# A GpSimd fill of 400 columns in place of 900 between pairs of indirect transfers

## The reference

```python
x = x + 0.5 * ffn(layernorm(x), gate_w, gate_b, w1, b1, w2, b2)
x = x + attn(layernorm(x), Wq, Wkv_down, Wk_up, Wv_up, Wo)
x = x + 0.5 * ffn(layernorm(x), gate_w, gate_b, w1, b1, w2, b2)

def ffn(x, ...):                      # 8 experts, 2 of them for each token
    probs = softmax(x @ gate_w.T + gate_b)
    topk_vals, topk_idx = top_k(probs, 2)
    h = relu(einsum('bsd,edh->bseh', x, w1) + b1)      # 256 hidden units
    expert_out = einsum('bseh,eho->bseo', h, w2) + b2
    return sum(expert_out[topk_idx] * topk_vals)

def attn(x, ...):                     # 8 heads of 32 features, softmax over 512 keys
    ...
```

## Time and profile before

| | us |
|---|---|
| median of 3 runs | 1219.44 |
| lowest and highest | 1216.77 and 1219.60 |
| the profiled execution | 1225.29 |
| its span, first to last instruction | 1223.5 |
| busy: PE | 1150.6 |
| busy: ACT | 958.0 |
| busy: DVE | 724.7 |
| busy: POOL | 678.9 |

### The profile page before, as it was taken

One profiled execution on the slowest core, in us unless ns is written; L12 is line 12 of the kernel. 1 busy time (PEld: TensorE's weight loads), 2 busy tenths in 40 slices (PEclk: granted clock), 3 DMA queues, 4 the chain that ended last, 5 costly groups with the idle time before them and its releaser, 6 DMA issues.

```text
span 1223.5 us, 25810 instructions
## 1 busy us (share of the span) xinstructions
PE 1150.6 (94%) x8142; PEld 762.4 (62%) x8142; DVE 724.7 (59%) x2254; ACT 958.0 (78%) x2383; POOL 678.9 (55%) x768
## 2 busy tenths in 40 slices
PE   7989898999989989999999999999999999999896
PEld 3666576666666545676666665665766446667575
DVE  4775438666496745665555867555756636647245
ACT  4457748789898898997888888898989888888532
POOL 2035548537370887803876777881820884257646
PEclk8977888799999979999999998999999989999988
DMA  8056546456574115655677645567652144676872
GB/s 279 10 206 192 162 144 193 126 156 202 158 214 147 55 39 177 208 172 157 200 215 228 194 139 164 186 201 206 183 157 60 41 151 125 182 214 176 250 253 80
DMA packets 159882, 202.05 MB, mean 165 GB/s; under 512 B 16938, under 2 KB 103426, under 8 KB 159747
## 3 DMA queue, kind: packets, MB, share of 16 engines
q1 hardware_dynamic: 144196, 168.90, 44.8%
q0 software_dynamic: 15360, 31.49, 8.9%
q10 hardware_dynamic: 192, 0.02, 0.0%
HBM read 152.50 MB, written 47.84 MB: 164 GB/s over the span
## 4 chain that ended last, share of the span: by engine, by line
PE 68%; ACT 20%; DVE 4%; issue 3%; POOL 3%; DMA 2%; SPq 0%; POOLq 0%; ACTq 0%; DVEq 0%
PE psum L1568 63%; ACT probs L1173 7%; ACT psum L1182 6%; PE psum L1686 2%; DVE neg_m L1522 2%; POOL Y L1100 2%; ACT xnC L1138 1%; DMA wt<-packed 1%; ACT xnA L1138 1%; PE psum L1653 1%; ACT hg L1219 1%; POOL pause L1064 1%; ACT xnB L1138 1%; PE psum L1751 1%; ACT xg_T L1247 1%
## 5 line engine op out<-in xcount | busy, mean ns | idle before, releaser
L1522 DVE TENSOR_REDUCE neg_m<-psum 128x1 f32<-128x512 f32 x512 | 317.5, 685 | 189.4 <-PE psum L1568 188.9
L1568 PE MATMUL psum<-nat 32*128 32x512 f32 x2048 | 372.7, 667 | 2.8 <-ACT nat L1251 1.5
L1182 ACT ACTIVATE psum<-psum,neg_m 128x512 f32<-128x512 f32 x512 | 340.9, 681 | 34.5 <-DVE neg_m L1522 33.7
L1173 ACT ACTIVATE probs<-psum 128x512 f32<-128x512 f32 x512 | 266.0, 627 | 37.7 <-PE psum L1568 36.4
L1080 POOL DMA_INDIRECT slots_A<-xnA,posA x120 | 117.1, 976 | 197.9 <-DMA xs<-slots_A 64.3
L1100 POOL DMA_INDIRECT Y<-results_C,posC x120 | 115.4, 962 | 170.8 <-DMA results_C<-ys 130.9
L1064 POOL MEMSET pause<- 128x900 f32 x240 | 207.6, 865 | 0.1
L1568 PEld LDWEIGHTS psum<-xg_T,wt 128*128 128x128 f32 x1296 | 163.6, 200 | 49.7 <-ACT psum L1182 14.7
L1568 PEld LDWEIGHTS psum<-nat 32*128 32x128 f32 x2048 | 135.7, 191 | 91.7 <-issue 22.1
L1568 PE MATMUL psum<-xg_T,wt 128*128 128x128 f32 x1296 | 180.2, 290 | 7.4 <-DMA wt<-packed 3.3
L1568 PEld LDWEIGHTS psum<-wt,hg 128*128 128x128 f32 x1296 | 153.0, 193 | 27.6 <-ACT hg L1219 9.6
(11 more groups left out here) (190 smaller groups left out, 1374.9 us busy)
## 6 DMA issues: line engine op xcount, KB each, us to landing
wt<-packed SPq DMA_DIRECT2D x324, 320.0 KB, 4.0
xs<-slots_A SPq DMA_DIRECT2D x36, 256.0 KB, 4.3
results_A<-ys SPq DMA_DIRECT2D x36, 256.0 KB
xs<-slots_C SPq DMA_DIRECT2D x36, 256.0 KB, 4.4
results_C<-ys SPq DMA_DIRECT2D x36, 256.0 KB
X<-in_L_attn_x_dram SPq DMA_DIRECT2D x16, 256.0 KB, 8.0
out_dram<-X SPq DMA_DIRECT2D x16, 256.0 KB, 3.9
packed<-probs SPq DMA_DIRECT2D x1, 2560.0 KB, 9.0
```

Source lines behind the costliest of these rows:

```text
L1173: act.activation(probs[:, kt, j, :], at.banks()[j][:], ACT.Exp).then_inc(a_done, 1)
L1182: act.activation(at.banks()[j][:], at.banks()[j][:], ACT.Exp, bias=neg_m[:, g, n, j:j + 1], accum_out=sums[:, g, n, j:j + 1]).then_inc(S[" ...
L1522: V_.tensor_reduce(neg_m[:, g, n, j:j + 1], at.banks()[j][:], AX.X, ALU.max, negate=True).then_inc(S["r_done"], 1)
L1568: return nc.tensor.matmul(dst, w, m, start=start, stop=stop)
```

## The change

The tile that `apart` fills has 400 columns instead of 900. The fill, the wait on its end, the order of all steps and every other wait stay as they are; the rows of PE, DVE and ACT are the same in both programs, and on POOL only the width of the fill differs.

```diff
         ident = sb("ident", [P, P])
-        pause = sb("pause", [P, 900])
+        pause = sb("pause", [P, 400])
         ones = sb("ones", [P, P])
```

## The result

| | before | changed |
|---|---|---|
| median, lowest to highest, us | 1219.52 (1216.77 to 1221.9, 4 runs) | 1212.24 (1211.77 to 1212.77, 4 runs) |
| ratio, 95% interval | | 0.9941 (0.9920 to 0.9963) |
| profiled execution, its span, us | 1225.29, 1223.5 | 1212.48, 1210.7 |
| mean granted clock of TensorE | 0.946 | 0.954 |
| the changed kernel once more, later, median, us | 1219.59 (33 runs) | 1215.43 (12 runs) |

The change makes the kernel faster, by 7.3 us in the first comparison and by 4.2 us in the second (0.5 to 7.8 us by the interval). The forecast was 2.5 us. Its range held both times; its likeliest outcome, the same, did not come. Four executions in the slow state are left out of all medians and ratios of the later comparisons.

The account below looks back on a forecast made before the run. PE was taken to bound the kernel, with 68% of the chain (POOL 3%). Terms of 1.45 and 1.0 us sum to 2.5 us less, 1219.44 to 1216.9 us; own range 1214.5 to 1219.0, wider range 1211.0 to 1222.5 us.

Parts of the forecast that it names:

- likeliest outcome, the same: Whole kernel: time between 1215.8 and 1223.1 us, not told from no change; chance 0.58.
- The fill and the pace: On POOL: fill 0.43 us shorter, its row 0.42 to 0.45 us; pace of pairs from 3.35 to 2.92 us.
- The rival that the pace does not change: On POOL: pairs held by their own transfers, whose rows grow by what the fill loses; 1219.4 us, chance 0.06.
- The first term, the end of the program: Last gather steps: gathers done 4.7 us earlier, but DVE's dense sum lets the last `comb` start only 1.45 us earlier.
- The part of the step on the last store of `results_C`: Last four gathers may wait for this store until 1201.7 us; last transfer still lands at 1214.7 us, ahead of DVE's 1215.24.
- The second term, the operations that the fill holds up: Small DVE operations on the chain held by transfer and fill: 1.0 us less, bounds 0 and 3.7 us.
- The square rule: DVE holds: lost time goes with the square of the hold's length, 1.4 to 0.95 us, leaving 0.46.
- the prediction's reading of the row at 878 us: DVE operation beside a first transfer of a pair, no fill directly behind: takes 0.17 us, so is not held.
- the halving: Holds on the chain: half of the 2.0 us taken, 1.0 us, since the second latest input may take over.
- the rows at 608 us: DVE operation of 1.40 us, starting 0.46 us into a second transfer, ending with the fill behind; read as the longer hold.
- The rivals on the clock: PE's low-clock stretch from 208 us disappears, 1211.4 us, chance 0.15; or a new one comes at 192 us, 1224.0 us, 0.13.
- The prediction's sign of being wrong: Longer indirect transfers, DVE still waiting at the end for gathered rows, or over 4 us change with the clock as it was.

Follow-up runs that it names:

- 900 columns and no holds: DVE's small one-operand operations rewritten with two tile operands, fill kept at 900 columns, against the kernel before: 1216.35 us, ratio 0.9964.

## Why the prediction was right in its range and short in its sum

**The fill and the pace** came as worked out: 448 ns, which is the value taken down from the 900 columns, and 2.93 us for the forecast's 2.92 us, with the transfers' rows unchanged. The rival that the pace does not change is out.

**The first term, the end of the program, was mis-sized: 1.45 us were forecast, 3.2 to 3.5 us measured.** The step that the prediction took was right as far as it went: the idle time of 1.47 us ahead of the last `comb` is gone, and DVE's own work is what is late next. What it missed is that the last row on the chain of waits is not the end of the program. The span ended with POOL's DRAIN, 2.2 us after SP had everything; with the faster POOL the DRAIN ends 1.0 us ahead of SP. So POOL's whole end counts down to the point where SP's takes over. In the two traces the end part is 4.6 us shorter: 1.5 us of DVE's idle time, 2.0 us (2.2 − 0.2) of SP's wait for the DRAIN, and the remaining 1.1 us because the dense sequence ended that much earlier after the last `shiftC`, which is scatter or a held operation less. The first two make 3.5 us, and 400 columns at the end alone took 3.2 ± 1.3 us less at equal clock. The other kernels confirm it on both sides: with 900 columns at the end alone the end part is 61.6 us again, 1300 bring it to 65 and 66 us with POOL last, and from 500 columns down it stops falling, since SP is last. The part of the step on the last store of `results_C` was right too: the last gathers wait 1.4 us for it, and it costs nothing.

**The second term, the operations that the fill holds up, came out larger as well: 1.0 us was forecast, 1.9 to 2.8 us are the best values measured.** The mechanism was right: with 900 columns and no holds the time falls by 1.9 ± 1.3 us at equal clock, with 1300 by 5.6 ± 1.6 us. That 1.0 us was too small is likely but not shown, since it lies inside the first interval (0.6 to 3.1 us). One factor of the term was wrong for certain, the share of held time that is left. The square rule with (0.95 / 1.4)² gave 46%; the traces show 6.9 of 33.9 us, 20%. The rule took the hold to run through the last half microsecond of the transfer and then the fill. With 900 columns it does; with 400 an operation caught in the transfer is let go at the transfer's end. At 187 us of the changed kernel:

```profile
187.20 0.97 POOL L1080 DMA_INDIRECT slots_A<-xnA,posA  x1 [0.31 <-issue]
187.44 0.69 DVE L1354 TENSOR_SCALAR shiftA<-shiftA 128x4 f32<-128x4 f32 x1
188.16 0.45 POOL L1064 MEMSET pause<- 128x400 f32 x1
```

It ends at 188.13 us, where the fill only begins. So there are two short windows in the place of one long one: 0.69 − 0.17 = 0.52 us in the transfer, and the fill's 0.45 us. The same square rule with them gives (0.52² + 0.45²) / (1.58 − 0.17)² = 24%, close to the 20% measured. The rule was sound, and its 0.95 us was wrong. (A first transfer of a pair holds too, against the prediction's reading of the row at 878 us: in before, 8 of the 50 held operations start 0.53 us or more after the start of a first transfer and end with it. The row at 878 us starts after 0.42 us.)

The other factor is what a hold on the chain is worth. The prediction counted four of them, 3.7 us, and halved what the rule said would go. On the chain of the changed kernel three such pieces of more than 0.3 us are left:

```profile
336.91 0.66 DVE neg_hl L1541
...
452.30 0.35 DVE neg_hl L1541
...
1101.08 0.50 DVE shiftC L1354
```

They hold 1.0 us, where before has 3.7 us in the prediction's four and 0.4 us in two shorter ones (at 203 and 340 us), so the chain gave up 3.1 us. With 80% of 3.7 us gone, the halving would make 1.5 us and no halving 3.0 us; the 1.9 ± 1.3 us at equal clock fits either, and the 2.8 us of the fit the second. So whether the halving was right stays open. Counted by all held time instead of by the chain, a held microsecond costs 0.06 to 0.12 us at equal clock (1.9 of 33.9 us, 5.6 of 48.6 us), and 0.10 us by the fit.

The terms measured add up to 5 to 6 us. The four kernels with 400 columns or fewer throughout show 3.7 to 4.6 us at equal clock, with 1.2 to 1.6 us to either side, so one term or both may lie at the low end. The first comparison's 7.3 us holds some 3 us more, which go with its four executions at a high clock. As far as these runs show, that is luck and not the change.

**The rule of the Trainium skill** ("SBUF — State Buffer", section "Who interferes with whom"), that whoever comes first keeps the shared ports for its whole instruction, would have left a quarter of the lost time if the fill alone held DVE. The prediction weighed that against the longer hold in the rows at 608 us and went by the rows. With 400 columns the measured 20% is nearer to that rule's quarter than to the 46%: there, a fill holds up only what comes during it or just ahead of it, though the transfer holds as well. At 900 columns the rule by itself does not describe the rows, as a hold passes from the transfer into the fill. On which operations are held the traces agree with it: casts and tensor-scalar operations took up to 1.58 us, and none of the 166 is held in the two-operand form.

**The rivals on the clock** did not come at the places given for them. The changed kernel's windows around 192 and 208 us, beside the earlier trace rows:

```profile
192.00:196.00 4.00, 4.00 (x39) 3.96 (x41) 0.88 (x2) 3.70 (x12) 3.21 (x4) 1.00 0.31 106
204.00:208.00 4.00, 4.00 (x11) 1.81 (x10) 3.62 (x17) 4.00 (x13) 3.42 (x5) 0.61 0.85 270
208.00:212.00 4.00, 4.00 (x18) 2.94 (x19) 2.57 (x6) 1.73 (x8) 3.15 (x5) 0.50 1.00 317
```

The stretch at 1.2 GHz from 208 us is still there, and at 192 us there is no new one. The mean clock rose from 0.946 to 0.954, but it was 0.949 in the second trace of the same kernel. In the middle part PE was at 1.2 GHz for 105.3 us before and for 88.9 and 107.8 us in the two traces after. So the low clock moved the first comparison, but as something that varies from execution to execution at many places of the program; that it did so by the mechanism of either rival no trace shows. The prediction's sign of being wrong, more than 4 us with the clock as it was, is not met by the first comparison, where the clock rose.

**The chances.** Faster had 0.30. The forecast of 2.5 us lay just inside what can't be told from no change (3.7 us), and the gain at equal clock, about 4 us, lies just outside, so the short first term was enough to turn the outcome. The second comparison's 4.2 us fall into the forecast's own range (1214.5 to 1219.0 us). The first one's 1212.24 us do not: the wider range held them only because it took in the price of a clock rival whose mechanism did not come.

## What to carry to other kernels

Look at the program's last instructions, each engine's own DRAIN and what SP waits for there, before you say what ends the program: the chain of waits ends at the last work. Here POOL's DRAIN ended 9.2 us after the start of the last indirect transfer's row, so an engine that looked done was the one that set the end.

Where an operation of DVE shows a minimum and median of 0.17 us and a maximum ten times that, put its start beside POOL's rows; if it is held there, either shorten POOL's fill or write the operation with two tile operands. Its cost here was about a tenth of the sum of the held time.

Where executions of one kernel spread more than the change is worth, put each time beside its mean granted clock, for both kernels, before you explain the difference.

## What was unexpected about the hardware

- POOL's DRAIN took 10.68 to 10.78 us in all 14 traces, from 8 to 1300 columns, although its last indirect transfer had landed 2.62 us after it began. What it does in that time no row shows.
- A hold that begins in a second transfer more than 0.3 us ahead of its fill runs on through the fill with 900 and 1300 columns and with two fills of 450, never with 400 or 500, and in 4 of 15 cases with 700. The cause is open.
- The form of a DVE operation decides whether it is held: 161 to 170 ns for each scalar_tensor_tensor of `veps` and `shift`, beside the same POOL work with which a tensor_scalar took up to 1.58 us. An operation of any form that comes right behind a held one is late with it: the scalar_tensor_tensor of line 1427, usually 0.16 us, took 1.04 us at 83.17 us of before, behind the held `gateA` of line 1425.
